# Layer 1's attention with its negative row maxima carried inside the queries

## The reference

```python
x = x + pos_emb[:S][None]
w = xp.reshape(B, nW, WIN, H, hd)                     # WIN = 64, H = 16, hd = 8
attn = softmax(einsum('bnqhd,bnkhd->bnhqk', w, w) * scale, axis=-1)
local = einsum('bnhqk,bnkhd->bnqhd', attn, w)
comp = conv_general_dilated(x.T, conv_w, window_strides=(4,)) + conv_b      # 64 compressed tokens
gt = concatenate([comp, broadcast_to(global_memory, (B, G, D))], axis=1)    # 128 global keys
ga = softmax(einsum('bshd,bghd->bhsg', xm, gt) * scale, axis=-1)
glob = einsum('bhsg,bghd->bshd', ga, gt)
mix = sigmoid(concatenate([local, glob], -1) @ gate_w + gate_b)
out = (mix * local + (1.0 - mix) * glob) @ out_w + out_b
```

## Time and profile before

| what | value |
|---|---|
| median of 3 runs | 1383.09 us (1370.75 to 1385.61) |
| the profiled execution | 1381.65 us, its span 1379.8 us |
| busy in the span | PE 82%, PEld 49%, DVE 58%, ACT 36%, POOL 42% |
| mean granted PE clock | 0.891 of full speed |
| chain that ended last | PE 49%, DVE 4%, issue 3%, DMA 1%, ACT 1% |
| matmul groups of layer 1's attention in that chain | L2211 5%, L2154 4%, L2108 3%, L2161 3%, L2191 2%, L2120 2%, L2193 2%, L2180 2% |

### The profile page before, as it was taken

The page is one execution under the profiler, slowest core; times in us unless marked ns, Lnnn a source line. Parts: engine busy times, 40 slices in busy tenths (PEclk is TensorE's granted clock), DMA queues, the critical chain, the costliest instruction groups (busy, mean ns, idle before and its releaser), DMA issues.

```text
span 1379.8 us, 20897 instructions
## 1 busy us (share of the span) xinstructions
PE 1130.8 (82%) x6836; PEld 680.3 (49%) x6836; DVE 797.3 (58%) x2040; ACT 502.4 (36%) x1137; POOL 585.9 (42%) x708
## 2 busy tenths in 40 slices
PE   2778788766659994799999999999942899999990
PEld 1356555555335662446546546555631455555550
DVE  2488888888522222434656866756454455665565
ACT  0334444433325652133343443343410344434440
POOL 0257777777514554512233554442353123222321
PEclk9999999998669997578999999999955999999995
DMA  7676776572144222101101111001112511111106
GB/s 290 152 179 157 170 179 154 140 162 79 36 144 165 79 77 66 57 9 36 37 26 47 53 39 49 28 28 28 37 33 71 171 32 36 34 39 32 38 18 190
DMA packets 96047, 117.28 MB, mean 85 GB/s; under 512 B 11176, under 2 KB 81320, under 8 KB 92984
## 3 DMA queue, kind: packets, MB, share of 16 engines
q1 hardware_dynamic: 86984, 97.46, 26.5%
q0 software_dynamic: 8704, 17.97, 4.0%
q10 hardware_dynamic: 256, 0.53, 0.2%
HBM read 85.35 MB, written 32.17 MB: 85 GB/s over the span
## 4 chain that ended last, share of the span: by engine, by line
PE 49%; DVE 4%; issue 3%; DMA 1%; POOL 1%; SPq 1%; ACT 1%; POOLq 0%; DVEq 0%; ACTq 0%
PE bank L1969 9%; PE bank L2211 5%; PE bank L1955 4%; PE bank L2154 4%; PE bank L2108 3%; PE bank L1979 3%; PE bank L2161 3%; PE bank L2191 2%; PE bank L2120 2%; PE bank L1963 2%; PE bank L2193 2%; PE bank L2180 2%; PE bank L2225 1%; PE bank L2176 1%; PE bank L1739 1%
## 5 line engine op out<-in xcount | busy, mean ns | idle before, releaser
L1156 POOL DMA_INDIRECT slots<-pay,slot x128 | 128.7, 1005 | 82.3 <-issue 72.2
L1171 POOL DMA_INDIRECT y<-region,xin x80 | 76.9, 961 | 193.4 <-ACT region L1533 173.0
L1969 PE MATMUL bank<-wgl,rows 128*128 x288 | 138.7, 604 | 5.8 <-ACT rows L1516 5.8
L972 DVE TENSOR_REDUCE rows<-bank 128x4 f32<-128x512 f32 x128 | 79.5, 683 | 74.5 <-PE bank L2108 74.2
L1516 ACT ACTIVATE rows<-bank 128x256 f32<-128x256 f32 x216 | 80.9, 383 | 101.9 <-PE bank L1963 100.8
L1171 POOL DMA_INDIRECT y<-hh,region x64 | 61.3, 957 | 119.7 <-ACT hh L1533 105.1
L727 DVE TENSOR_TENSOR rows<-bank,w0uv 128x512 f32<-128x512 f32 x72 | 49.7, 691 | 95.9 <-PE bank L1969 86.9
L1652 ACT ACTIVATE w0uv<-bank 128x512 f32<-128x512 f32 x128 | 66.1, 602 | 88.5 <-PE bank L2161 88.5
L719 DVE TENSOR_TENSOR rows<-region,bank 128x256 f32<-128x256 f32 x72 | 30.3, 421 | 115.3 <-ACT region L1521 115.3
L1963 PEld LDWEIGHTS bank<-consts,rows 128*128 128x128 f32 x432 | 58.0, 143 | 74.1 <-issue 50.5
L1194 POOL TENSOR_TENSOR region<-region 128x512 f32<-128x512 f32 x64 | 83.1, 1311 | 13.7 <-DVE region L859 11.9
(11 more groups left out here) (320 smaller groups left out, 2410.7 us busy)
## 6 DMA issues: line engine op xcount, KB each, us to landing
region<-vrdram SPq DMA_DIRECT2D x16, 1024.0 KB
region<-vrdram SPq DMA_DIRECT2D x32, 512.0 KB, 8.8
xin<-slots SPq DMA_DIRECT2D x80, 65.0 KB
region<-slots SPq DMA_DIRECT2D x64, 65.0 KB, 1.9
wgl<-in_wgl SPq DMA_DIRECT2D x1, 4096.0 KB
rows<-y SPq DMA_DIRECT2D x8, 512.0 KB, 4.0
wgl<-y SPq DMA_DIRECT2D x8, 512.0 KB, 7.5
xres<-x SPq DMA_DIRECT2D x12, 256.0 KB, 2.3
```

The source lines that it names most:

```text
L972: V.tensor_reduce(maxg[:, t, g * QD:g * QD + HG], bank[g].rearrange("p (h k) -> p h k", h=HG), axis=AX, op=ALU.max).then_inc(S["c_mx"], 1)
L1156: p.indirect_dma_start(io["slots"], bass.IndirectOffsetOnAxis(ap=slot_of(l, b)[:, k, t:t + 1], axis=0), pay_of(l, b)[:, k, t, :], None).th ...
L1171: p.indirect_dma_start(io["y"], bass.IndirectOffsetOnAxis(ap=xins[par][:, h, k, P + 1:P + 2].bitcast(U32), axis=0), bYs[par][:, h, k, :], ...
L1969: ins = M(bank[k][:, :], bT[:, k, tile(c)], wgl[:, bass.ds(ex_of[h][k], 1), c, :].squeeze(1), start=c == 0, stop=c == FC - 1)
```

## The change

- The keys of the global scores come in two tiles. `gmk` (one buffer where there were two) holds them with the heads in reverse order of r (`mask4r`), and a second tile `gmk1`, made on ACT by `keys_again` (four 128 x 128 instructions), holds the keys of head r with one row of ones in a partition of another head of the group.
- `queries` makes four tiles of queries `xneg[r]` on DVE (128 x 512 each, from `bank[7]`, `negrow` and `xmk`): the masked queries of head r, with the negative maxima in the partition where `gmk1` has ones. One product `gmk1 x xneg` (L2181) then gives scores less maxima. `less_global` (four groups of four matmuls a row) and `less_max_global` are gone.
- `max_global` writes the maxima eight columns apart. `max_T_global(a)` is called for the next row, in the step before, ahead of `again_local(i, 1)`; it waits for `norm_global(i)`, and `attend_local(i, 0, 1)` waits for `queries(a)`, since both need bank 7.
- On PE the sections are written so that each exponential section follows the score section behind it: `score_local(i, 0)`, `again_global(i, 0)`, ..., `score_local(i, 1)`, `again_global(i, 1)`, ..., `score_global(a, 0)`, and so on. `turn_out(b, 0)` comes first in the step, straight behind `front_T`.
- On DVE `max_local(i, 1)` moves ahead of the router, the front of row f behind `max_global(a, 1)`, `mix(b)` ahead of `max_global(a, 2)`, `norm_global(i)` between `max_global(a, 2)` and `max_global(a, 3)`; `queries(a)` follows.
- `xneg` lies in `b12`, the biases of layer 1's experts. Their load (2 MB) moves from the end of layer 0 to the tail of the attention, behind the last exponential section.

```diff
+            def queries(b):
+                v.wait_ge(S["c_max_t"], 2 * b + 1)
+                v.wait_ge(S["c_xm"], b * HG + HG)
+                if b:
+                    v.wait_ge(S["c_E"], (b - 1) * E_STEPS + NHG * HG)
+                for r in range(HG):
+                    V.scalar_tensor_tensor(out=xneg[:, r, :], in0=bank[7], scalar=negrow[:, HG - 1 - r:HG - r], in1=xmk[b % 2][:, r, :],
+                                           op0=ALU.mult, op1=ALU.add).then_inc(S["c_neg"], 1)
...
+            def keys_again(b):
+                a.wait_ge(S["c_gm"], 2 * b + 1)
+                for r in range(HG):
+                    ins = A.activation(gmk1[:, r, :], gtT[:, :], ACT.Identity, scale=mask4[:, r:r + 1],
+                                       bias=mask32[:, DH * (HG - 1 - r):DH * (HG - 1 - r) + 1])
+                ins.then_inc(S["c_gm"], 1)
...
-                    M(bank[g], gmk[p][heads(g), r, :], xTs[p][heads(g), :], start=True, stop=False)
-            def less_global(b, r):
-                for g in range(NHG):
-                    M(bank[g], pick_g[heads(g), r, :], negmax[heads(g), :], start=False, stop=True).then_inc(S["c_E"], 1)
+                    M(bank[g], gmk1[heads(g), r, :], xneg[heads(g), r, :], start=True, stop=True).then_inc(S["c_E"], 1)
```

More of the change, by code:

```diff
@@ L133, in build @@
         mgb = wa0[:, NT, :]
-        gmk = [rows[:, 9 + i, :].rearrange("p (r k) -> p r k", r=HG) for i in range(2)]
-        negmax = rows[:, 11, :]
+        gmk, gmk1 = (rows[:, 9 + i, :].rearrange("p (r k) -> p r k", r=HG) for i in range(2))
+        xneg = b12[:, 0:4, :]
         maxg = rows[:, 5, :].rearrange("p (t c) -> p t c", t=NT)
@@ L1056, in step @@
                 if ok(a):
-                    max_global(a, 2)
+                    max_global(a, 3)
+                    queries(a)
+                if ok(f) and not ok(i):
+                    add_front(f)
+                    stats_front(f)
                 if ok(c):
                     modulate(c)
+                if ok(i):
+                    norm_local(i, 0, 0)
                 if ok(b):
                     residual(b)
-                if ok(i):
-                    norm_local(i, 0, 0)
-                if ok(a):
-                    max_global(a, 3)
                 if ok(i):
@@ L1678, in step @@
                 if ok(i):
-                    less_max_global(i)
+                    exps(i, 0)
                 if ok(b):
                     mixed_T(b, b % 2, 0)
-                if ok(i):
-                    exps(i, 0)
                 if ok(a):
@@ L2201, in attend_local @@
                     t_.wait_ge(S["c_ng"], b + 1)
+                    if t and b + 1 < NB:
+                        t_.wait_ge(S["c_neg"], (b + 1) * NEG_STEPS + HG)
                 elif t == 0:
@@ L2268, in step @@
                 if ok(i):
-                    less_global(i, 0)
+                    score_local(i, p, 0)
+                    again_global(i, 0)
                 if ok(a):
                     compress(a, a % 2)
-                if ok(i):
-                    score_local(i, p, 0)
                 if ok(b):
                     attend_local(b, 1, 1)
+                if ok(i):
+                    score_local(i, p, 1)
                 if ok(d):
@@ L2278, in step @@
                 if ok(i):
-                    again_global(i, p, 1)
-                    less_global(i, 1)
+                    again_global(i, 1)
                     attend_global(i, 0)
-                    score_local(i, p, 1)
+                if ok(a):
+                    score_global(a, a % 2, 0)
                 if ok(b):
@@ L2287, in step @@
                 if ok(i):
-                    again_global(i, p, 2)
-                    less_global(i, 2)
+                    again_global(i, 2)
                     attend_global(i, 1)
-                    max_T_local(i)
-                if ok(a):
-                    score_global(a, a % 2, 0)
-                if ok(i):
-                    attend_global(i, 2)
-                    local_values(i, p)
-                    again_global(i, p, 3)
-                    less_global(i, 3)
-                if ok(b):
-                    gate(b, b % 2)
                 if ok(a):
@@ L2303, in step @@
                 if ok(i):
+                    max_T_local(i)
+                    again_global(i, 3)
+                    attend_global(i, 2)
+                    local_values(i, p)
+                if ok(a):
+                    score_global(a, a % 2, 2)
+                if ok(b):
+                    gate(b, b % 2)
+                if ok(i):
+                    again_local(i, p, 0)
                     attend_global(i, 3)
-                    again_local(i, p, 0)
                 if ok(b):
```

83 lines of the change are left out of this document (45 added, 38 removed).

## The result

The changed kernel takes 1554.52 us, the median of 4 runs (1552.16 to 1556.14), against 1384.35 (1370.75 to 1386.85, 4 runs) for the kernel before: a ratio of 1.1254 [1.1211, 1.1297]. It is 170 us slower. Some kernels also had runs at a lower granted clock, over 1.5% longer than their fastest run (five of the eight of the kernel before on chip C of the experiments, one of the seven on chip B), and all medians and ratios here are of the other runs. The forecast was 1490 in a range of 1435 to 1525, so the direction was right and the size was not: the loss is 1.6 times the forecast one.

What follows compares the result with a forecast made beforehand. It took PE's work and the loop between score and exponential sections as the bound, with waits ruling the new row: 1381.65 + 96 (rows 1 to 6) + 7 (row 0) + 4 (ahead of it) + 1 (row 7) = 1490 us, range 1435 to 1525.

Steps and rivals of the forecast that it cites:

- half loops of 3.9 and 3.4 us: Attention loop through banks 0 to 3: score section's end to exponential section's end 3.9 us, exponential to score 3.4.
- parts 1 and 2: Row from score_local(i, 0)'s end to score_local(i, 1)'s, 8.2 us; then to again_global(i, 3)'s end, 18.5 us.
- The removed products: less_global on PE: four groups a row at 1.07 us each, 4.3 us a row saved.
- The two in-order waits: exps(i, 3) behind local_values on ACT, 7.1 us against 3.4; maxima behind mix(b) on DVE, 8.7 against 4.6.
- The rival in which they don't bind (1430): Waits behind local_values and mix(b) cost nothing extra: row 56 us, 59 with the clock, about 1430; chance 0.10.
- the rival by which PE's own stream is the bound (1348): PE's work sets the attention's time, each removed group saves 1.07 us, 34 in all, so 1348; chance 0.04.
- I take a share between, and 4.1 us a row for it: 67.8: Attention row: lower granted clock from PE's gaps adds 4.1 us to 63.7, giving 67.8; ends nothing and 8.
- the walk of 63.7: A middle attention row walked section by section in the new order: 63.7 us, against 51.7 for the old row.
- the upper end, 71 us a row: Attention rows if gaps between bursts bring the low clock level back: some 71 us a row.
- the clock stays low for whole rows: Rival: PE's 41.5 us a row nearly double, rows 80 us or more, 1580 and over; chance 0.07.
- Row 7 and behind: Last attention row, without next scores: loses 4.3 us of products, gains some waits, +1 us.
- parts 1 to 3: Row from score_local(i, 0)'s end through score_local(i, 1), again_global(i, 3) to score_global(a, 2)'s end: 8.2, 18.5 and 7.1 us.

Runs made afterwards that it cites:

- the kernel without the two waits: Changed kernel with mix(b) behind max_global(a, 2) on DVE and local_values(i, p) ahead of again_global(i, 3) on PE: 1474.84 us, ratio 1.0682.
- the three made from it on chip A: Changed kernel with seven zero groups a step, 1502.78 us; with mix(b) behind max_global(a, 2), 1505.61; with that and local_values ahead of again_global(i, 3), 1474.84.
- the two with the load in place: The kernel before, 1383 us on chip A, and the same with one zero group ahead of each less_global, 1414.14 us.
- one pair of kernels: On chip C, the changed kernel unedited, 1581.59 us, and with a zero group behind each again_global, 1602.56 us.

## Why the prediction was right, and where it was wrong

**What bounds the kernel, right.** The half loops of 3.9 and 3.4 us explain parts 1 and 2: at full clock they came out at 7.9 and 18.4 us against 8.2 and 18.5 walked. Where PE has less to do between two sections than the half loop lasts, as there, fewer products on PE can't shorten them.

**The removed products, right in size.** They were put at 4.3 us a row. In the old order, adding as many costs 31 us in all, of which some 8 may be one row's low clock, and the new products with the moved load save 40 (31 to 52), against 8 x 4.3 = 34.

**The added work, right.** `queries` 2.7 us a row against 2.8, `keys_again` 1.65 against 1 to 2.

**The two in-order waits, right.** Both stand in the trace where they were walked, and both go when the one call is moved that writes them. The rival in which they don't bind (1430) is refuted: with both really gone the kernel takes 1474.84, and with both in place 1554.52. So is the rival by which PE's own stream is the bound (1348) for this order. For the old order its price holds: there the same products give 0.971.

**The clock, wrong.** This is the step that failed: "I take a share between, and 4.1 us a row for it: 67.8. The ends are nothing and 8." The row took 76.75 us, so what lies over the walk of 63.7 is 13 us, three times the term taken and five above its upper end. Six times the missing 9 us is 54 of the 66 us. Two things were wrong in it. The share of the time at the low level was put between a tenth and the half of the stretch from 300 to 400 us, because the new row keeps PE busier than that stretch (its 56%). The stretch of rows 1 to 6 has PE busy 87% (399.78 of 460) and is at the low level in 58%. PE's busy share, which hides the waits inside a group, did not tell the clock here. Pauses of 2 to 3 us, three in the row shown, went with the low level, but so did a wait of 1.15 us with products let go one by one behind it, and the stretches behind both that PE worked through without rest ran at 0.50. And the prediction gives no working from a share of the time to 4.1 us. It left out that `gate`, `attend_local` and the score sections lie on the chain of waits, where the low level lengthens what the other engines wait for: `gate`'s 1.9 us became 3.8, and tanh, `mix`, maxima and `again_local` all moved behind it.

The Trainium skill, page TensorE: Matmul & The Clock Gate, part on HAM oscillation, was given in the prediction for the upper end, 71 us a row. The rows went the way it says, and 6 us further: 76.75 at 0.71. The gaps in that part's example are longer than the pauses here of 1.15 to 2.90 us, so that the low level came back behind these is this trace's finding and not that part's. The range's end of 1525 is also more than the prediction's own terms give: 1381.65 + 6 x (71.7 - 51.8) + 7 + 4 + 1 = 1513.

The rival "the clock stays low for whole rows", 1580 with rows of 80 or more, was the nearest in size: two of the six rows took 80. But as a mechanism it is not what happened. The clock stood at 0.93 in 20 us of the row shown, and six rows had it at 0.71, not at 0.50. The case between, low in more than half of each row, had no place among the rivals. A range that held it would have had to reach 1580.

**Row 7 and behind, wrong.** +1 was forecast, +13.2 measured. From the start of `score_local(7, 0)` to the end of `again_local(7, 0)` it is 34.3 us at a clock of 0.75, where it was 28.1 at 1.00, +6.2: the prediction gave row 7 the waits of parts 1 to 3, but not the low clock that comes with them. Another 7 lie behind that, up to the second `route` behind it (36.8 us against 29.8). There `attend_global(7, 3)` now stands behind `again_local(7, 0)`, and the reciprocal behind it is no longer covered: PE idles 3.35 us ahead of `attend_local(7, 0, 0)`, until L1002, where it idled 1.34 us for ACT's exponentials before. That is 2 of the 7 us; that the rest is the clock's is argued, not measured. From that `route` to the end it is 364.9 us in both, so the moved load costs nothing behind the attention, as was forecast.

**Row 0 and the prologue.** Row 0 was 13.2 longer instead of 7, with the clock at 0.67 where it was 0.79. The attention's start lost what was forecast: from DVE's first front instruction (below) to `score_local(0, 0)` it took 587.14 - 544.83 = 42.31 us and takes 584.97 - 538.32 = 46.65, +4.3 against +4. But the layer started earlier. First front instruction on DVE, kernel before and kernel after:

```profile
544.83 0.69 DVE L769 TENSOR_TENSOR rows<-rows 128x512 f32<-128x512 f32 x1 [11.70 <-DMA wam<-mods]
```

```profile
538.32 0.69 DVE L773 TENSOR_TENSOR rows<-rows 128x512 f32<-128x512 f32 x1 [11.77 <-DMA wam<-mods]
```

That is 6.5 us earlier. The load of `b12` no longer stands at the end of layer 0, and the prediction priced its move at nothing without looking at the side that it leaves. But the changed kernel and the three made from it on chip A began layer 1 between 536.91 and 541.75, so 5 us of spread lie in a stage in which they don't differ; the two with the load in place began at 544.17 and 544.83. And on chip C the changed kernel itself began it at 547.35. So the earlier start may be the moved load or no more than the spread between executions; no run tested it alone.

**What stays open.** What a removed group of products is worth in the new order (0.66 us by one pair of kernels). How much filling brings to the kernel without the two waits, 1 us a row or several. What it is in a row that brings the low level back, since once no more than a wait of 1.15 us stood ahead of it. And the share of the 13 us a row that would remain at a clock of 1.00 throughout: no kernel here got the new order above 0.89.

## What to carry to other kernels

Change what is computed and the order in which it is issued in two steps, each with its own time: here the first was worth 2.9% and the second cost 16%. When a new order opens pauses on PE, price them twice, once by their length and once for the work behind them that may then run at half speed; here a row walked at 64 us came out 13 us longer, although PE was busy in 87% of the time. And to see how much of a loss is the clock's, fill the pauses with products that add zero: if the kernel becomes faster by doing more, some of the loss was the clock's.

## What the runs showed of the hardware

- Seven groups a row of matmuls with zero weights, into a bank that doesn't change by them, raised the mean granted clock of six rows from 0.71 to 0.85 and took 52 us off; fifteen raised it from 0.70 to 0.89 and took off 71 us, on another chip.
- Behind a pause of 2.04 us PE worked 15 of 16 us on products of 34 columns and scores, and the granted clock was 0.50 through all of it. Behind a wait of 1.15 us in the same row it was 0.50 too, in 6 of 6 us busy (826 to 832).
- One kernel takes 1383, 1422 and 1411 us on three chips. The changed kernel's ratio to it came out alike in two comparisons, on different chips: 1.1254 and 1.1225.
